# An opening with head strips first, a second head group of strips, and twenty unread products on TensorE

## The reference, cut to what matters

```python
x = L0_attn_x                                  # (8, 512, 128)
mod = (_silu(L0_c) @ L0_wmod).reshape(8, 6, 1, -1)
sa, ca, ga, sb, cb, gb = (mod[:, i] for i in range(6))
ga = (2 * (ga >= 0) - 1) * jnp.maximum(jnp.abs(ga), 0.25)      # gb likewise
h = _layernorm(x) * (1 + ca) + sa
x = x + ga * attn(h)      # 16 heads of 8; Wq, Wk, Wv, Wp are mean(|W|) * sign(W) by row
h = _layernorm(x) * (1 + cb) + sb
x = x + gb * ffn(h)       # shared gated FFN, and top 2 of 8 experts by sigmoid router
```

## Time and profile before

| | us |
|---|---|
| median of 3 runs | 667.86 |
| lowest, highest | 663.66, 669.41 |
| profiled execution | 667.02 |
| its span | 665.2 |

### The profile page before, as it was taken

How to read it: one execution, slowest core, us unless ns; L and a number is a source line. 1 busy time by engine, 2 the same in 40 slices (tenths; PEclk the granted TensorE clock), 3 DMA queues, 4 the chain that set the end, 5 groups by cost and what they waited for, 6 DMA issues and landing times.

```text
span 665.2 us, 10688 instructions
## 1 busy us (share of the span) xinstructions
PE 615.2 (92%) x3461; PEld 288.7 (43%) x3461; DVE 504.9 (76%) x1065; ACT 404.1 (61%) x791; POOL 259.2 (39%) x309
## 2 busy tenths in 40 slices
PE   4899999999999999999999999999999589886997
PEld 2332324233333333423333333232378578776855
DVE  5779788889988989888998888988467534433567
ACT  2345777777777776777778778678735224433431
POOL 4240041414352451434336235025056656566610
PEclk9969999999999999999999999999999988997999
DMA  3443332442541445344244244214832223222155
GB/s 103 134 121 117 117 114 98 132 131 90 160 123 64 133 134 134 109 149 116 93 147 127 69 133 130 67 50 135 226 81 57 68 65 88 63 68 61 56 185 195
DMA packets 58828, 73.91 MB, mean 111 GB/s; under 512 B 10857, under 2 KB 39819, under 8 KB 58772
## 3 DMA queue, kind: packets, MB, share of 16 engines
q1 hardware_dynamic: 53144, 63.30, 32.0%
q0 software_dynamic: 4320, 8.47, 3.7%
q10 hardware_dynamic: 1308, 1.46, 0.8%
HBM read 38.36 MB, written 34.96 MB: 110 GB/s over the span
## 4 chain that ended last, share of the span: by engine, by line
PE 73%; DVE 12%; ACT 7%; issue 3%; another core or an unknown queue 2%; DMA 1%; SPq 1%; POOL 1%; ACTq 1%; DVEq 0%; POOLq 0%
PE pv L1620 15%; PE st L1609 15%; PE mx L1594 14%; PE mx L1806 7%; DVE neg_max L1077 6%; PE st L1820 5%; PE mx L1754 3%; PE misc L1487 2%; PE misc L1514 2%; PE st L1770 2%; ACT pt L868 2%; PE pv L1794 1%; PE misc L1520 1%; DVE stats_sb L1026 1%
## 5 line engine op out<-in xcount | busy, mean ns | idle before, releaser
L868 ACT ACTIVATE pt<-st 128x512 f32<-128x512 f32 x496 | 282.1, 598 | 105.8 <-PE st L1609 95.9
L1077 DVE TENSOR_REDUCE neg_max<-mx 128x2 f32<-128x1024 f32 x248 | 294.5, 1215 | 47.9 <-PE mx L1594 44.6
L1620 PE MATMUL pv<-pt,vs 128*32 128x512 f32 x1024 | 136.4, 605 | 0.3 <-ACT pt L868 0.3
L745 POOL DMA_INDIRECT routed<-rec,row_u x64 | 64.1, 1002 | 136.6 <-PE pv L1620 114.8
L812 POOL DMA_INDIRECT results<-qs,home_u x71 | 72.0, 1014 | 50.8 <-ACT qs L995 28.4
L1609 PE MATMUL st<-even_qk 74*128 74x512 bf16 x256 | 89.0, 389 | 1.9 <-ACT pt L868 1.1
L1609 PE MATMUL st<-qs,ks 74*128 74x512 bf16 x240 | 81.4, 383 | 1.8 <-ACT pt L868 1.1
L1594 PE MATMUL mx<-ks,qs 72*128 72x512 bf16 x256 | 76.5, 380 | 2.9 <-DVE neg_max L1077 2.5
L1594 PE MATMUL mx<-even_qk 72*128 72x512 bf16 x240 | 74.5, 393 | 4.4 <-DVE neg_max L1077 4.1
L437 POOL TENSOR_TENSOR qk_r<-qk_f,qk_parts 128x512 f32<-128x512 f32 x15 | 17.4, 1161 | 98.8 <-DVE qk_parts L429 98.7
L1609 PEld LDWEIGHTS st<-even_qk 74*128 74x128 bf16 x256 | 20.9, 99 | 71.5 <-ACT pt L868 51.7
(11 more groups left out here) (217 smaller groups left out, 798.0 us busy)
## 6 DMA issues: line engine op xcount, KB each, us to landing
routed<-pad_rows SPq DMA_DIRECT2D x64, 260.0 KB
even_qk<-q_parts SPq DMA_DIRECT2D x48, 96.0 KB
qs<-q_parts SPq DMA_DIRECT2D x48, 96.0 KB
ks<-k_parts SPq DMA_DIRECT2D x48, 96.0 KB
even_qk<-k_parts SPq DMA_DIRECT2D x42, 96.0 KB
ks<-routed SPq DMA_DIRECT2D x28, 130.0 KB
q_parts<-qk_parts SPq DMA_DIRECT2D x21, 128.0 KB
k_parts<-qk_parts SPq DMA_DIRECT2D x7, 384.0 KB, 2.3
```

Of the source, the lines that this page charges most:

```text
L745: pool.indirect_dma_start(out=routed_dram, out_offset=bass.IndirectOffsetOnAxis(ap=row_u[:, k, t:t + 1], axis=0), in_=rec[b.par][:, k, t, ...
L868: act.activation(pt[n % 2][:, hh, :], score_bank(b, n, hh), ACT.Exp, scale=SCALE).then_inc(exp_done, 1)
L1077: dve.tensor_reduce(neg_max[g % 2][:, hh, 2 * half:2 * half + 2], mx_bank[half][:], AX_X, ALU.max, negate=True).then_inc(mx_free, 1)
L1620: last = pe.matmul(pv_bank[32 * hh:32 * (hh + 1), :], vs[b.par][:, j, HG * g + hh, :], pt[n % 2][:, hh, :], start=(n % Y_SLOTS == 0), stop ...
```

## The change

- `DIRECT` is 2, and `DIRECT_FILLS` 12: group 1 of batch 0 gets strips too, and its first four fills (8 to 11, its first two heads) use them. The other four use the stack.
- TensorE projects the strips before the q projection, and the fills follow the k projection. The strips of group 1 are projected after fill 5; `max_T` comes after fill 7, ln1_T of batch 1 after fill 8, its q projection after fill 9.
- 20 products of a tile of ones (128x512 bf16, in `scratch[1]`) are issued at five places of TensorE's opening: 7, 5, 4, 2 and 2. They are written to `mx_bank[1]` and read by nobody.
- SP loads the q and k biases before Wv and Wp, and x of batch 1 before the other small loads. `spread_bias` waits for the q and k biases alone. The wait for group 1's stack and the m rows is gone; x of batch 2 is loaded after group 1's stacks.
- POOL splits q as well as k, before rstd of batch 1 and most constants.
- ScalarE issues the ones later, v's eviction stands before the k stores, it loads only group 0's k stack, and issues the m rows before hT of batch 1.
- VectorE normalises batch 1 after the eighth maximum.

```diff
-DIRECT = 1
-DIRECT_FILLS = DIRECT * 2 * HG
+DIRECT = 2
+DIRECT_FILLS = 3 * HG
...
+        busy_ops = scratch[1][:, 0:T // 2]
...
-        BEFORE = ["c", "mod", "ln1_0", "q_0", "k_0", "v_0", "ln1_1", "q_1", "m0", "k_1"]
+        BEFORE = ["c", "mod", "ln1_0", "q_0", "k_0", "v_0", "m0", "ln1_1", "q_1", "k_1"]
...
         def _(sp):
             sp.dma_start(x_in[:], x[0].rearrange("(p t) c -> p t c", p=P)).then_inc(x_in_loaded, 16)
-            for i, w in enumerate((Wq, Wk, Wv, Wp)):
-                sp.dma_start(w_nat[:, i, :], w).then_inc(w_loaded[i // 2], 16)
-            for i, v in enumerate((bq, bk, bv)):
-                sp.dma_start(bias_qkv[:, i:i + 1], v.rearrange("(p o) -> p o", o=1)).then_inc(small_loaded, 16)
+            for i, w in enumerate((Wq, Wk)):
+                sp.dma_start(w_nat[:, i, :], w).then_inc(w_loaded[0], 16)
+            for i, v in enumerate((bq, bk)):
+                sp.dma_start(bias_qkv[:, i:i + 1], v.rearrange("(p o) -> p o", o=1)).then_inc(qk_bias_loaded, 16)
+            for i, w in enumerate((Wv, Wp)):
+                sp.dma_start(w_nat[:, 2 + i, :], w).then_inc(w_loaded[1], 16)
...
+            load_x(B1)
+            sp.dma_start(bias_qkv[:, 2:3], bv.rearrange("(p o) -> p o", o=1)).then_inc(small_loaded, 16)
...
-            load_x(B1)
             sp.wait_ge(parts_ready, 1)
             store_q_heads(0, HG, first_stored[0])
             store_q_heads(HG, H, q_stored)
-            load_x(B1.plus(1))
             sp.wait_ge(first_stored[0], 16 * PARTS)
             load_q_stack(B0, 0)
-            load_q_stack(B0, 1)
-            sp.wait_ge(stack_loaded[0][1], STACK_DMAS)
-            sp.wait_ge(m_row_loaded[0], ROW_DMAS)
-            for g in (2, 3):
+            for g in (1, 2, 3):
                 load_stack(B0, g)
+                if g == 1:
+                    load_x(B1.plus(1))
...
+            split_qk(pool, B0, 0)
+            split_qk(pool, B0, 1)
+            rstd(mv1, ve1, var1_ready, rstd1, rstd1_ready, stats1_ready, B1)
...
             pool.wait_ge(setup_pool, 4)
-            rstd(mv1, ve1, var1_ready, rstd1, rstd1_ready, stats1_ready, B1)
-            split_qk(pool, B0, 1)
             fill_values(pool, 1)
...
-            act.wait_ge(setup_pool, 3)
-            for i in range(2):
-                load_ones(act, i)
...
-            act.wait_ge(small_loaded, 80)
-            evacuate_qk(B0, 0, use(AHEAD, "q_0"))
             act.wait_ge(first_done, 1)
             evacuate_direct(1, 0, 3)
             evacuate_direct(0, 0, 4)
+            evacuate_qk(B0, 0, use(AHEAD, "q_0"))
             evacuate_qk(B0, 1, use(AHEAD, "k_0"))
+            act.wait_ge(setup_pool, 3)
+            load_ones(act, 0)
             evacuate_wT(2, 5)
             act.activation(exp_first[:], strip_rows[:], ACT.Exp)
+            act.wait_ge(v_ready[0], 2)
+            evacuate_v(B0, use(AHEAD, "v_0"))
             act.wait_ge(parts_ready, 2)
...
-            act.wait_ge(v_ready[0], 2)
-            evacuate_v(B0, use(AHEAD, "v_0"))
+            evacuate_direct(1, 1, 6)
+            evacuate_direct(0, 1, 7)
             act.wait_ge(key_ones[0], 16)
             load_k_stack(act, B0, 0)
-            load_k_stack(act, B0, 1)
-            project_in(B1, use(AHEAD, "ln1_1"))
-            evacuate_qk(B1, 0, use(AHEAD, "q_1"))
+            act.wait_ge(small_loaded, 48)
             act.wait_ge(misc_free, use(AHEAD, "m0") + 1)
...
+            project_in(B1, use(AHEAD, "ln1_1"))
+            evacuate_qk(B1, 0, use(AHEAD, "q_1"))
+            load_ones(act, 1)
             evacuate_qk(B1, 1, use(AHEAD, "k_1"))
...
+            dve.memset(busy_ops, 1.0).then_inc(busy_ready, 1)
...
             first_part(dve, B0, 0, use(AHEAD, "q_0"))
-            split_qk(dve, B0, 0)
+            maxima(range(1))
+            first_part(dve, B0, 1, use(AHEAD, "k_0"))
+
+            maxima(range(1, 2 * HG))
+            split_max(B0, 0, use(AHEAD, "m0"))
             layer_norm1(B1)
-            first_part(dve, B0, 1, use(AHEAD, "k_0"))
-
-            maxima(range(DIRECT_FILLS))
-            split_max(B0, 0, use(AHEAD, "m0"))
-            maxima(range(DIRECT_FILLS, FIRST_FILLS))
+            maxima(range(2 * HG, FIRST_FILLS))
...
+            def keep_busy(count):
+
+                ones = busy_ops.bitcast(BF16)
+                for _ in range(count):
+                    pe.matmul(mx_bank[1][:, 1, :], ones[:, 0:P], ones, start=True, stop=True)
+
+            pe.wait_ge(busy_ready, 1)
+            keep_busy(7)
...
             pe.transpose(misc[:, B:B + E], router_nat[:], ident[0:E, 0:E]).then_inc(misc_full, 1)
+            keep_busy(5)
             free(use(AHEAD, "mod"))
...
-                        pe.wait_ge(first_done, (4,)[g])
+                        pe.wait_ge(first_done, (4, 7)[g])
...
-                if hh == 0 and half == 0:
+                if hh == 0 and half == 0 or fill == DIRECT_FILLS:
                     pe.wait_ge(stack_loaded[b.par][g], STACK_DMAS * (b.half + 1))
...
-                pe.wait_ge(small_loaded, 80)
+                pe.wait_ge(qk_bias_loaded, 32)
...
+            keep_busy(4)
             ln1_T(B0, use(AHEAD, "ln1_0"))
             spread_bias()
+            keep_busy(2)
             weights_T(0)
-            pe.wait_ge(first_done, 2)
+            keep_busy(2)
+            free(use(AHEAD, "q_0"))
+            project_direct(1, 0, 2)
+            project_direct(0, 0, 2)
             project(0, use(AHEAD, "q_0"))
-            project_direct(1, 0, 1)
-            project_direct(0, 0, 2)
             project(1, use(AHEAD, "k_0"))
...
                 if fill == 5:
+                    project_direct(1, 1, 4)
+                    project_direct(0, 1, 4)
+                if fill == 2 * HG - 1:
+                    max_T(B0, 0, use(AHEAD, "m0"))
+                if fill == 2 * HG:
                     ln1_T(B1, use(AHEAD, "ln1_1"))
-                if fill == DIRECT_FILLS - 1:
+                if fill == 2 * HG + 1:
                     project(0, use(AHEAD, "q_1"))
-                    max_T(B0, 0, use(AHEAD, "m0"))
             project(1, use(AHEAD, "k_1"))
```

More of the change, by code:

```diff
@@ L213, in adaln_block @@
         strips_ready = sem("strips_ready")
+        busy_ready = sem("busy_ready")
         first_stored = [sem(f"first_stored{i}") for i in range(2)]
         small_loaded = sem("small_loaded")
+        qk_bias_loaded = sem("qk_bias_loaded")
         c_loaded = sem("c_loaded")
@@ L484, in _, with load_x @@
             sp.dma_start(x_in[:], x[0].rearrange("(p t) c -> p t c", p=P)).then_inc(x_in_loaded, 16)
-            for i, w in enumerate((Wq, Wk, Wv, Wp)):
-                sp.dma_start(w_nat[:, i, :], w).then_inc(w_loaded[i // 2], 16)
-            for i, v in enumerate((bq, bk, bv)):
-                sp.dma_start(bias_qkv[:, i:i + 1], v.rearrange("(p o) -> p o", o=1)).then_inc(small_loaded, 16)
+            for i, w in enumerate((Wq, Wk)):
[4 more added lines that the diff above has]
+                sp.dma_start(w_nat[:, 2 + i, :], w).then_inc(w_loaded[1], 16)
+            def load_x(b):
+                sp.wait_ge(ln1_ready, TT * b.n)
+                sp.dma_start(x_in[:], x[bass.ds(b.n, 1)].rearrange("o (p t) c -> p (o t) c", p=P)).then_inc(x_in_loaded, 16)
+            load_x(B1)
+            sp.dma_start(bias_qkv[:, 2:3], bv.rearrange("(p o) -> p o", o=1)).then_inc(small_loaded, 16)
             sp.dma_start(bp_bc[:], bp.partition_broadcast(P)).then_inc(small_loaded, 16)
@@ L694, in _ @@
             rstd(mv1, ve1, var1_ready, rstd1, rstd1_ready, stats1_ready, B0)
[L695 to L716, removed]
             def residual(b):
@@ L769, in scatter @@
                     scatter_rows(b, i)
+            split_qk(pool, B0, 0)
+            split_qk(pool, B0, 1)
+            rstd(mv1, ve1, var1_ready, rstd1, rstd1_ready, stats1_ready, B1)
+            pool.affine_select(out=earlier_token[:], in_=ones_bf[:], compare_op=ALU.is_gt, fill=0.0, base=0,
+                               pattern=[[1, P]], channel_multiplier=-1).then_inc(consts_ready, 1)
+            pool.memset(marks[:], 0.0).then_inc(consts_ready, 1)
+            pool.sem_inc(rows_free, 2)
+            pool.iota(expert_no[:], pattern=[[1, E]], base=0, channel_multiplier=0,
+                      allow_small_or_imprecise_dtypes=True).then_inc(consts_ready, 1)
+            pool.iota(next_row[0][:], pattern=[[REGION, E]], base=0, channel_multiplier=0,
+                      allow_small_or_imprecise_dtypes=True).then_inc(consts_ready, 1)
+            for k in range(RING):
+                pool.memset(digit[:, k:k + 1], float(E ** k)).then_inc(consts_ready, 1)
+            pool.memset(pad_rows[:], 0.0).then_inc(pad_ready, 1)
+            pool.wait_ge(pad_ready, 1)
+            pool.memset(pad_rows[:, :, C + 1], float(FAR)).then_inc(pad_ready, 1)
+            pool.iota(first_row[:], pattern=[[REGION, E]], base=0, channel_multiplier=0,
+                      allow_small_or_imprecise_dtypes=True).then_inc(consts_ready, 1)
```

(8 more changed lines are left out.)

3 lines of the change are left out of this document (removed).

## The result

The changed kernel takes 675.59 us (median of 4 runs, 674.7 to 677.12) against 667.29 us (4 runs). The ratio recorded from these runs is 1.0151, with a 95% interval of 1.0116 to 1.0185; the two medians alone stand at 1.0124, inside it. The forecast was 664.8, and its range ended at 669.5. The profiled execution spans 673.0 us against 665.2.

What follows compares the result with a forecast made beforehand. TensorE was taken to bound the kernel (92% busy), VectorE nearly as full. Slot 0 at 37.1 plus 11.6 put fill 17 at 48.7 against 50.75, taken as 2.2 us: 667.0 - 2.2 = 664.8 us, range 658.5 to 669.5.

Steps and rivals of the forecast that it cites:

- The opening: Start of kernel to first fill: early biases and products lift the clock; fill 0 at 15.2 instead of 18.46, 3.3 us gained.
- The eight fills: First eight direct fills: VectorE waits twice, 0.7 and 1.3 us; eighth maximum at 28.4 against 30.23, 1.8 us left.
- Does the clock hold?: After the fills: clock falls near 30, returns 3.5 to 5.5 us after dense work; 2.1 us lost, slot 0 at 37.1.
- The page: Skill page on TensorE's clock: drops feared only after longer idle gaps, so clock stays up and slot 0 comes at 35.0.
- my own rule: Clock after the fills: it falls again near 30 because TensorE idles 2.3 us with one transpose and one fill between.
- To slot 0: Eighth maximum to slot 0: transposes, normalisations, fills and projections from 28.4 to 35.0, before any clock fall.
- rival 1: Clock stays up through the fills: slot 0 at 35.0, fill 17 at 46.6, 4.2 us gained, 662.8; chance 0.25.
- Slots 0 and 1: Slot 0 to the end of fill 17: VectorE bounds them at the higher level, 11.6 us against 13.1, 1.5 us gained.
- The slower one: Opening: products don't lift the clock before the strips; fill 17 at 52.3, 1.5 us late, 668.5; chance 0.08.
- the anchor: End of fill 17's maxima, 50.75 before: where it ends earlier, the rest moves with it, both engines being nearly full.
- the sum: Fill 17 at 37.1 + 11.6 = 48.7 against 50.75: 2.1 us, taken as 2.2, giving 664.8 us.

Runs made afterwards that it cites:

- open128: Changed kernel with 40 unread 128-row products at TensorE's very start instead of 7; spacing 0.43 us, then 0.22; 11.13 us for all, kernel time not given.
- hold128: Changed kernel with 15 more unread 128x512 products of ones, all 128 rows, between the first fills; 0.9986 of the kernel before.
- holdearly: Changed kernel with four unread 128-row products behind fills 0, 1 and 2 only; 1.0079 of the kernel before, median 670.25 us.
- best: Changed kernel with 11 unread full-height products between fills and batch 1's normalisation, transposes and q projection back before the eighth maximum's transpose; 0.9996 of the kernel before.
- best3: Kernel before plus early q and k biases with a wait for them alone, 20 opening products and 16 full-height products between fills; 0.9947, 661.12 us.
- open32: Changed kernel with 40 unread 32-row products at TensorE's very start instead of 7; 3 or 4 per us for all 17 us, kernel time not given.
- best2: As best, but SP waits again for the first m rows before loading batch 2's x and groups 2 and 3; 0.9942 of the kernel before.
- beforeprod: Kernel before with the 20 opening products alone, at the corresponding five places; 1.0003 of the kernel before.
- beforehold: Kernel before with 16 unread full-height products between its first fills and in its two idle gaps, none in the opening; 0.9964 of the kernel before.

## Why the prediction was wrong

**The opening** was right: biases at 8.56, clock up before 7.2 us (forecast 4.7 to 6.7), strip pass 1.07, fill 0 at 15.01, first maximum at 16.18 against 16.3. open128 gives the rise by itself, 4.7 us after the start.

**The eight fills** were sized within 1.4 us while the clock was up. In hold128 the eighth maximum ends at 29.75 and in holdearly at 28.93, against 28.4 forecast. In the changed kernel it is 34.19.

**"Does the clock hold?" is the step that failed**, in three ways. The fall came at 20.5, not near 30: I weighed only the two gaps near 30, and the ones before the fall (0.78 us in front of the k projection at 13.95, 0.49 in front of fill 3 at 19.08) I passed over. From 15.0 to the fall stood four 32-row fills, one transpose of weights and the start of project_v; four full-height products there were enough to keep the level (holdearly). An idle gap isn't enough for a fall either: best idles 1.11 us in front of slot 0 and best3 0.95 at 30.76, and the level held. Whether gap or rows made the fall stays open. The return took 34 us, not 3.5 to 5.5: I took it from two places where the dense work had full height, and applied it to "dense work" of any kind. holdearly shows 31 us from a fall at 29 alone. open32 shows that products of 32 rows alone can stay at the lower level, but 17 of the 31 us in holdearly, and all of the kernel before's 13.7, stand without any; what decides when the level returns stays open. And the price was read as half of 4.3 us; the term was 2.1 us, and hold128 prices it at 12.2 us at fill 17 (60.42 - 48.19) and 1.6% of the time. The rows to suspect it were there: from 35 to 44 us the kernel before was at 0.5 while TensorE was busy throughout; I had used only the two ends of that stretch.

**The page.** The Trainium skill (TensorE: Matmul & The Clock Gate, "Why this matters for your kernels") would have had no fall; the trace had one after gaps of 0.78 and 0.49 us. It was the less apt guide of the two, and my own rule stood on the same ground: idle time.

**To slot 0.** With the clock high, slot 0 comes at 36.77 (hold128) and not at 35.0. Of these 1.8 us 1.35 stand already at the eighth maximum (29.75), and TensorE then works without a gap up to slot 0. So even rival 1, which had this case, was too bright: fill 17 is 2.6 us ahead of the kernel before, not 4.2, and the time shows no clear gain. The m rows' DMA doesn't hold slot 0 in hold128, but it is next: where the steps ahead of it are shorter, it costs 1.2 us (best 37.10, best2 35.89), and I had named SP's removed wait only as time gained.

**Slots 0 and 1** were priced at 11.6 us at the high level; hold128 has 11.4 (36.77 to 48.19), best2 11.4. In the changed kernel they took 14.8 (45.6 to 60.4), three fifths of it at the lower level.

**The rivals.** The slower one had the sign but neither the place nor the size: it put the lower level in the opening, which was the sound part, and at 1.5 us. None of the four had the clock falling and staying down. The shift of fill 17 did reach the end but for 1.8 us, as the anchor said. In the sum 50.75 - 48.7 is 2.05; the 2.2 taken for it is a slip of 0.15 us.

## What to carry to other kernels

A low clock is not only a matter of long gaps: a few full-height unread products between TensorE's first fills were worth more than three times their price (12.2 us for 3.3). A busy engine is no sign that the level will come back: it stayed low for 17 us of unbroken work in holdearly. Price a fall by how long the level has stayed low elsewhere in the same trace, not by the shortest return. Work that is moved forward runs into waits sooner, and each wait on an engine that looks idle may be what keeps bulk DMAs off a small urgent one: undo such waits one at a time.

## What the runs showed that I had not expected

The same kernel before took 641.62 us on one chip and 664.8 to 667.6 on the others. The first 490 us take nearly the same time: POOL's last modulation starts at 493.6 in best (that chip) and at 492.5 in best2. The rest took 145 us there and 169 here. In best's trace the clock is 1.00 throughout this last part, in best2's it falls three times. These are two kernels, but they differ in one wait. Which comes first, shorter waits or the level, wasn't tried.

One execution is not a law for the low stretch either: holdearly's profiled run took 675.22 us and its median is 670.25; beforeprod's stretch lasted from 32.1 to 52.6 in its slowest run, where before's lasted 31 to 44.7, at the same median time. The spread of 663.66 to 669.41 us of the kernel before may come from this. With the clock held it was 3.5 us in best2 and 6.2 in best3, against 7.2 of the kernel before on their chip, and 3.7 in beforehold but 9.4 in best, against 6.4, so that stays open.
